# Four graph layers on one core: when the destination one-hots are written, and where the edge features are multiplied in

## The reference, cut

```
x = LN(x + gin(x))      # 3 x: agg = segment_sum(x[src], dst); two 64x64 linears
h = relu(concat(x[src], edge_attr) @ W1 + b1)          # 64+32 -> 128, per edge
h = h @ W2 + b2
agg = segment_sum(h, dst) / max(count(dst), 1)         # scatter_mean
x = LN(x + relu(concat(x, agg) @ W3 + b3) @ W4 + b4)   # the edge network
x = LN(x + attention(x, src, dst))                     # softmax over a node's edges
x = LN(x + relational(x, src, dst, type, weight))
```

## Time and profile before

| | |
|---|---|
| median of 3 runs | 1974.95 us (1972.48 to 1977.16) |
| profiled execution | 1974.92 us, of which the span is 1973.6 us |
| filing, POOL's last indirect DMA | ends at 609 us |
| preparation with layer one's first aggregation | 594 to 918 us |
| layers one to three, rest | to 1065 us |
| edge network | 1080 to 1370 us |
| attention | 1377 to 1690 us |
| relational layer | 1700 to 1973 us |
| busy over the span | PE 65%, DVE 50%, POOL 41%, ACT 31% |

### The profile page before, as it was taken

The page is one execution under the profiler, slowest core; times in us unless marked ns, Lnnn a source line. Parts: engine busy times, 40 slices in busy tenths (PEclk is TensorE's granted clock), DMA queues, the critical chain, the costliest instruction groups (busy, mean ns, idle before and its releaser), DMA issues.

```text
span 1973.6 us, 48209 instructions
## 1 busy us (share of the span) xinstructions
PE 1286.1 (65%) x20479; PEld 1175.4 (60%) x20480; DVE 979.0 (50%) x2196; ACT 618.1 (31%) x1433; POOL 806.2 (41%) x883
## 2 busy tenths in 40 slices
PE   6410000000002777778998999998799998989897
PEld 2300000000001666667897999998799998888896
DVE  7200020000001455554447555655788888888986
ACT  4000000000001777774213444343566666300000
POOL 1777777777772000000001444441010010388896
PEclk7555555555555999999997999998899999899999
DMA  7610000001102999997665788874666661344442
GB/s 230 241 35 15 15 15 14 13 14 48 34 14 75 349 357 359 352 346 272 239 253 198 279 302 310 312 293 176 255 242 238 224 244 52 141 165 158 170 177 89
DMA packets 89277, 360.69 MB, mean 183 GB/s; under 512 B 24940, under 2 KB 38431, under 8 KB 82079
## 3 DMA queue, kind: packets, MB, share of 16 engines
q1 hardware_dynamic: 75744, 349.84, 47.9%
q0 software_dynamic: 13312, 7.69, 1.7%
HBM read 250.77 MB, written 106.68 MB: 181 GB/s over the span
## 4 chain that ended last, share of the span: by engine, by line
PE 38%; another core or an unknown queue 22%; DVE 14%; issue 11%; ACT 7%; DMA 3%; POOL 2%; SPq 2%; ACTq 0%; DVEq 0%; POOLq 0%
PE ps L2923 8%; PE ps L2575 6%; PE ps L2911 6%; PE ps L3189 5%; PE ps L3542 4%; DMA arena<-recs 2%; DVE arena L2354 2%; PE ps L3556 2%; ACT arena L2479 2%; ACT arena L2531 2%; DVE arena L3607 2%; SPq L2264 2%; PE ps L2459 1%; POOL arena L3598 1%
## 5 line engine op out<-in xcount | busy, mean ns | idle before, releaser
L2174 POOL DMA_INDIRECT recs<-arena x416 | 425.6, 1023 | 173.2 <-issue 131.8
L2981 POOL CAST arena<-arena 128x512 f32<-128x512 bf16 (+1 forms) x175 | 119.2, 683 | 627.1 <-DMA arena<-hot_out 457.6
L2302 DVE TENSOR_TENSOR arena<-arena 128x25 f32<-128x25 int32 x25 | 4.9, 196 | 415.9 <-DMA arena<-recs 391.7
L3542 PE MATMUL ps<-arena 125*128 125x64 bf16 x5850 | 191.7, 194 | 8.8 <-issue 8.7
L2459 PE MATMUL ps<-wz,arena 32*128 32x128 f32 x1248 | 58.8, 319 | 208.9 <-ACT arena L2479 113.9
L3542 PEld LDWEIGHTS ps<-arena 125*128 125x128 bf16 x5850 | 186.5, 98 | 10.4 <-issue 9.9
L2923 PE MATMUL ps<-arena 128*128 128x125 f32 x1300 | 182.2, 282 | 0.0
L2459 PEld LDWEIGHTS ps<-wz,arena 32*128 32x128 f32 x1248 | 49.2, 215 | 221.1 <-ACT arena L2479 119.6
L3067 DVE TENSOR_TENSOR arena<-ps,arena 128x512 f32<-128x512 f32 (+1 forms) x175 | 114.3, 653 | 118.7 <-PE ps L2911 115.6
L3014 ACT ACTIVATE arena<-arena 128x512 f32<-128x512 f32 (+1 forms) x175 | 105.1, 601 | 171.8 <-DVE arena L3067 171.8
L2923 PEld LDWEIGHTS ps<-arena 128*128 128x128 f32 x1300 | 158.8, 192 | 0.0
(11 more groups left out here) (380 smaller groups left out, 2480.5 us busy)
## 6 DMA issues: line engine op xcount, KB each, us to landing
arena<-ids_out SPq DMA_DIRECT2D x100, 832.0 KB, 6.2
arena<-hot_out SPq DMA_DIRECT2D x75, 832.0 KB, 6.2
arena<-e_out SPq DMA_DIRECT2D x25, 1664.0 KB, 6.9
arena<-adj_out SPq DMA_DIRECT2D x41, 800.0 KB, 6.8
e_out<-arena SPq DMA_DIRECT2D x25, 1024.0 KB
hot_out<-arena SPq DMA_DIRECT2D x25, 832.0 KB, 7.6
adj_out<-arena SPq DMA_DIRECT2D x25, 800.0 KB, 5.8
e_out<-arena SPq DMA_DIRECT2D x25, 640.0 KB
```

Of the source, the lines that this page charges most:

```text
L2174: nc.gpsimd.indirect_dma_start(out=recs, out_offset=bass.IndirectOffsetOnAxis(ap=slot_row[:, t:t + 1], axis=0), in_=rec_in[:, t, :], in_of ...
L2981: nc.gpsimd.tensor_copy(hot_e[s % NH][:, 0:len(js), :], hot_in[d % 2][:, js[0]:js[0] + len(js), :])\
L3542: ins = M(bank(step % 4, C, k * C), hot_r[d % 2][r][0:NP_, j * SLOTS:(j + 1) * SLOTS], px3[:, block_of(d, j), piece, r * C:(r + 1) * C], s ...
```

## The change

1. *Destination one-hots early.* A new pair `sp_hot_ahead` and `dve_hot_ahead` goes over all 25 blocks while POOL still files: load the records once more, make the destination one-hots (26 tiles in one instruction), store them in `hot_out`. It stands in step 1 of SP's and DVE's streams, ahead of the load of block 2, and starts when half of the edges are filed, since its buffers lie over the first half of `rec_in`. The store of `hot_d` in the steps goes; DVE still makes `hot_d` there for the adjacency.
2. *Features stored instead of their product.* The halves L2459, their evictions, `e1_out` and the late product of block 24 go. The transposed features (448 KB a block) are stored in `attr_out`. ACT packs the next block's features after the fourth adjacency group instead of after all seven. The adjacencies rotate over four banks.
3. *Edge network.* PE adds the features' product into the same PSUM bank as the gather, in K=32 float32 matmuls of `attr_in` (`pe_sums`). Four steps are now issued together, in four rounds: up to four feature products on different rows, then the gathers of these tiles. ACT applies relu straight from PSUM, DVE splits the result into three parts (two subtractions a step), and PE sums by destination with the bf16 one-hot as weights and 3x128 columns moving. DVE reduces the three parts and scales, PE transposes, ACT copies into `agg`. POOL's casts go.

```diff
@@ sp_shadow
-                    while ahead < NA and ahead + 2 <= d and (ahead + 1) * NT * SLOTS // 2 <= filed:
+                    while ahead < NA and ahead + 2 <= d:
+                        if ahead == 0:
+                            for half in range(2):
+                                sp.wait_ge(sem(f"hot_stored{half}"), 16 * (NT // 2 + 1 - half))
...
+                if step == 1:
+                    sp_hot_ahead(sp)
...
-                    sp.wait_ge(sem("hot"), 3 * d + 3)
-                    sp.dma_start(hot_out[d], hot_d[d % 2].rearrange("p j n -> p (j n)"))\
-                        .then_inc(sem(f"hot_stored{d % 2}"), 16)
...
-                    if d < NT - 1:
-                        sp_e1(sp, d)
+                    sp.wait_ge(sem("attr_turned"), d + 1)
+                    sp.dma_start(attr_out[d], attT[d % 2]).then_inc(sem(f"attr_stored{d % 2}"), 16)
@@ new
+        def sp_hot_ahead(sp):
+            for c in range(2 * QUARTER // CHUNK - 2, 2 * QUARTER // CHUNK):
+                sp.wait_ge(sem(f"filed{c % 2}"), 16 * CHUNK * (c // 2 + 1))
+            for d in range(NT + 1):
+                if d < NT:
...
+                    if d >= 2:
+                        sp.wait_ge(sem("hot_ahead"), d - 1)
+                    sp.dma_start(dst_rec[d % 2], block_rows(d)).then_inc(sem(f"dst_in{d % 2}"), 16)
+                if d >= 1:
+                    sp.wait_ge(sem("hot_ahead"), d)
+                    sp.dma_start(hot_out[d - 1], hot_ahead[(d - 1) % 2].rearrange("p j n -> p (j n)"))\
+                        .then_inc(sem(f"hot_stored{(d - 1) % 2}"), 16)
@@ act_shadow
-                    if d < NT - 1:
-                        act_e1_half(act, d, 0)
-                        act_pack(act, d + 1)
-                        act_e1_half(act, d, 1)
+                        if g == 3 and d < NT - 1:
+                            act_pack(act, d + 1)
@@ pe_edge2
-                if step < G7:
...
-                    if step >= 4:
-                        pe.wait_ge(sem("e1_added"), step - 3)
...
+                if step < G7 and step % 4 == 0:
+                    pe_sums(pe, step)
...
-                    pe.wait_ge(sem("dst_hot"), s + 1)
-                    pe.wait_ge(sem("act_relued"), s + 1)
+                    pe.wait_ge(sem("act_low"), s + 1)
...
-                        ins = M(bank(4 + d % 2, NP_), act_out[s % 4][:, k * HID:(k + 1) * HID],
-                                hot_e[s % NH][:, k, 0:NP_], start=j == 0, stop=j == NT, skip_group_check=True)
+                        ins = M(bank(4 + d % 2, PIECES * HID)[0:NP_, :], hot_in[d % 2][:, j, 0:NP_],
+                                x[:, :, k * HID:(k + 1) * HID], start=j == 0, stop=j == NT, skip_group_check=True)
...
+                    if step == turn_step(d):
+                        pe.wait_ge(sem("agg_scaled"), d + 1)
...
+        def turn_step(d):
+            return 7 * (d + 1) + LAG + 2
@@ pe_sums: waits
+            pe.wait_ge(sem("src_hot"), d + 1)
+            pe.wait_ge(sem(f"attr_in{d % 2}"), 16 * (d // 2 + 1))
+            if first:
+                pe.wait_ge(sem("act_relued"), first)
@@ dve_edge2
-                    V.tensor_tensor(pre[step % 2][:, 0:m], bank(step % 4, m),
-                                    e1_in[d % 2][:, 4 * g * HID:4 * g * HID + m], ALU.add).then_inc(sem("e1_added"), 1)
+                    dve.wait_ge(sem("act_relued"), step + 1)
+                    V.tensor_tensor(x[:, 1, 0:m], x[:, 0, 0:m], hi(x[:, 0, :])[:, 0:m], ALU.subtract)\
+                        .then_inc(sem("act_left"), 1)
+                    dve.wait_ge(sem("act_left"), step + 1)
+                    V.tensor_tensor(x[:, 2, 0:m], x[:, 1, 0:m], hi(x[:, 1, :])[:, 0:m], ALU.subtract)\
+                        .then_inc(sem("act_low"), 1)
...
+                    V.tensor_reduce(agg_sum, bank(4 + d % 2, PIECES * HID)[0:NP_, :]
+                                    .rearrange("p (t f) -> p f t", t=PIECES), AX, ALU.add).then_inc(sem("agg_summed"), 1)
...
+                    V.tensor_scalar(agg_mean[d % 2], agg_sum, deg[:, 2, d:d + 1], None, ALU.mult)\
+                        .then_inc(sem("agg_scaled"), 1)
```

More of the change, by code:

```diff
@@ L283, in build @@
         e1_in0_at = e2_at.at
-        e1_in = [e2_at([128, SB * HID]) for _ in range(2)]
+        attr_in = [e2_at([128, 7 * SLOTS]) for _ in range(2)]
+        act_out += [e2_at([128, PIECES, 4 * HID])]
+        assert e2_at.at <= e1_in0_at + SB * HID
+        e2_at.at = e1_in0_at + 2 * SB * HID
         src_hot_at = e2_at.at
@@ L287, in build @@
         rcp_at = e2_at.at
-        rcp_row = [e2_at([128, CH * NP_]) for _ in range(2)]
+        agg_sum, agg_mean = e2_at([NP_, HID]), [e2_at([NP_, HID]) for _ in range(2)]
+        e2_at.at = rcp_at + 2 * CH * NP_
         p3_at = e2_at.at
@@ L291, in build @@
         assert e2_at.at >= sh.at
-        pre = [e2_at([128, 4 * HID]) for _ in range(2)]
+        e2_at.at += 2 * 4 * HID
         low_end, high_end = e1_at.at, e2_at.at
@@ L2325, in dve_shadow @@
                         .then_inc(sem("seg_made"), 1)
+                if step == 1:
+                    dve_hot_ahead(dve, chain)
                 if 2 <= step <= NT + 1:
@@ L2816, in hid_step, with px_sums @@
         def hid_step(c):
-            return 7 * (tiles(c)[-1] + 1) + LAG + 2
+            return 7 * (tiles(c)[-1] + 1) + LAG + 4
+        def turn_step(d):
+            return 7 * (d + 1) + LAG + 2
+        def px_sums(first):
+            cells = [(s, (s - first + i) % 4) for i in range(4) for s in range(first, min(first + 4, G7))]
+            cells = [(s, k) for s, k in cells if k < len(groups(s // 7)[s % 7])]
+            last = {s: at for at, (s, k) in enumerate(cells)}
+            done, at = [0] * len(cells), 0
+            for s in sorted(last):
+                at = max(at, last[s])
+                done[at] += 1
+            return cells, done
         OUT, EVICT, ROOT, SCALED, TURN, TURNED, HUP, HIGH, LEFT, MID, LOW = 3, 4, 9, 11, 13, 15, 17, 19, 21, 23, 25
@@ L3010, in act_edge2 @@
                     m = HID * len(groups(d)[g])
[L3011 to L3014 removed]
+                    act.wait_ge(sem("px_got"), step + 1)
+                    if step >= 5:
+                        act.wait_ge(sem("act_summed"), step - 4)
+                    A(act_out[step % 5][:, 0, 0:m], bank(step % 4, m), ACT.Relu)\
+                        .then_inc(sem("act_relued"), 1)
+                for d in range(NT):
+                    if step == turn_step(d):
+                        act.wait_ge(sem("agg_turned"), d + 1)
+                        A(agg[:, d * NP_:(d + 1) * NP_], bank(4 + d % 2, NP_, PIECES * HID), ACT.Copy)\
+                            .then_inc(sem("agg_read"), 1)
                 for c in range(NCH):
```

246 lines of the change are left out of this document (99 added, 147 removed).

## The result

The changed kernel takes **2062.2 us** (median, 2053.4 to 2069.2) against 1973.9 of the kernel before in the same call: ratio 1.044, interval 1.041 to 1.046, slower. The forecast was 2026 us with a range of 1958 to 2072. The profiled execution is 2053.4 us with a span of 2051.6.

What follows compares the result with a forecast made beforehand. It took filing as bound by POOL, the preparation by transfers and their loop, the edge network by PE. The sum 1974.9 - 32.8 - 6.1 + 88.5 + 2 = 2026.5 was said as 2026 us, range 1958 to 2072.

Steps and rivals of the forecast that it cites:

- Filing: While POOL files edges: making 25 destination tables on DVE costs POOL about 6 us, ends 0 and 12.
- The rival in which POOL waits for each whole table: Filing: POOL waits while DVE makes each table, +41 us, 2067 us; chance 0.03.
- Head start of block 2: Start of the preparation: block 2's adjacency is stored at 639.3 instead of 649.0, -10 us.
- Period: Preparation: 10.7 us a block instead of 11.92, ends 10.2 and 11.5; counted as 23.5 us saved.
- the loop named: Preparation: load landing, ACT's pack, last three evictions, adjacency store, then the next load; sum 10.4 us, taken as 10.7.
- The rival at 8.5 us a block: Preparation: landings are hidden from ACT, a loop of 17 us for two blocks decides; 1978 us; chance 0.10.
- Late product: Block 24's 14 float32 matmuls, which stood on the chain, go: -6.1 us.
- PE's own work in the edge network: Edge network: PE's work without waits is 12.33 us a block, 1.09 more than before.
- the lone round: Edge network: a round of feature products alone among full-height gathers costs 0.41 us, 7 rounds a block, 2.87 us.
- The sums: Edge network: PE's sums by destination, 384 columns a tile, take 0.164 us a tile, 4.26 a block.
- Waits: Edge network: new PE waits of 2.45 us a block (ends 0.4 and 3.5), transpose 1.55, source table 0.5, estimated rest 0.4.
- The clock: Edge network rival: granted clock falls to a mean of 0.90 as PE pauses, +34 us, 2060 us; chance 0.12.

Runs made afterwards that it cites:

- e4: The changed kernel with ACT packing the next block's features behind all seven adjacency evictions; 2033.7 us, ratio 1.030 to before.
- e7: The changed kernel with the transpose two steps later, the source table one step earlier and the pack behind all adjacency evictions; 1965.3 us on a chip of the second sort.
- e5: The kernel before with only the destination one-hots made and stored while edges are filed; 1949.2 us, ratio 1.166 to before on its chip.
- e6: The changed kernel with SP loading the records one block earlier, ahead of the adjacency store of the block before; 1979.4 us on a chip of the second sort.
- e1: The changed kernel with the transpose of the block's mean two steps later in the order; 2017.3 us, ratio 1.021 to before.
- e3: The changed kernel without feature products in the edge network and without the waits between their rounds; 1982.8 us, ratio 1.003 to before.
- e9: The kernel of e5 with SP loading the records one block earlier; 1950.5 us.
- e12: The kernel before, unchanged, run once more with a profile on another chip; 1669.5 us.

## Why the prediction was right

The direction, the place and the mechanism held: the gain in the preparation, the larger loss in the edge network, PE idle there behind DVE's scaling and source table. The size was low by 36 us (27 by the profiled execution).

- **Filing.** +6 forecast, +1.2 came (609.20 for 607.96), and that it came so near is luck. The price of 1 us of POOL for 8 of DVE, from one place, was too low: a table beside POOL's DMAs costs it more than half its own length. A table and the POOL issue beside it, after, and an issue of before:

```profile
353.71 1.89 DVE L2294 TENSOR_TENSOR arena<-iota,arena 128x3328 bf16<-128x3328 bf16 x1
```

```profile
353.78 2.67 POOL L2182 DMA_INDIRECT recs<-arena  x1 [0.30 <-issue]
```

```profile
477.33 1.09 POOL L2174 DMA_INDIRECT recs<-arena  x1 [0.31 <-issue]
```

After, 32 of the 416 issues take more than 1.00 us, together 28.5 us over the usual 0.97, each of them beside work of DVE. 25.5 of these stand beside the 24 tables made while POOL files (45.5 us). Before, 176 issues took more than 1.00 us, together 24.9, most of them 1.09 like the one shown and beside no DVE work at all, and nine longer pauses added 5.4. These are gone after, so the end moved little; why they are gone isn't shown. The rival in which POOL waits for each whole table didn't come in the time (+41), but more than half of what it says of a table did.
- **Head start of block 2.** -10 forecast, -3.6 came (645.44 for 649.03). "Block 1 is nearly through when the filing ends" was wrong: its adjacency is stored at 635.36. ACT's pack, which stands in front of block 1's last evictions, waits until 627.02 for the load that SP issues at 621.58, behind `sp_hot_ahead`, and the last evictions come only at 634.97. The load isn't all of it: e4, with the pack behind the evictions, stores block 1 at 635.21, where ACT's last evictions again come late, and e7, the same there on a chip of the second sort, at 619.12.
- **Period.** 10.7 forecast, (871.85 - 645.44) / 22 = 10.29 came, and the loop named was the right one: ACT waits for the load in front of the pack, and e4 and e6 take that wait away and gain. Altogether -39.4 against -32.8. With e5 it can be divided: of the 1.6 us of a block 0.3 go with the one-hots' transfers and the remaining 1.3, by difference, with the product, its loop and the other changes there. I had counted the bytes of both and seen the loop, but not which of the two the loop hung on. The rival at 8.5 us a block wasn't what the change does, but e6 shows 7.6 once the load is moved, so its loop of 17 us for two blocks was priced too high.
- **Late product.** -6.1 forecast, 48.2 - 39.4 = 8.8 came between the last adjacency and the edge network.
- **PE's own work in the edge network.** 12.33 forecast, 13.25 measured (e7). The mis-sized term is the lone round: 0.41 taken, 0.54 measured, 0.91 us a block. I had taken the 0.18 us for getting in and out of a long stretch for that of a lone round, which is 0.31 (0.54 - 0.23). Why it is more isn't shown. The sums were right: 0.164 us a tile forecast, 1.36 us for eight seen (0.17).
- **Waits.** 2.45 forecast, about 40.2 / 24 = 1.7 measured: transpose 1.2 for 1.55, table 0.36 for 0.5, relu 0.1.
- **The clock**, a rival of 0.12, came in part beside the forecast: 0.95 in the edge network. 13.25 / 0.95 is 0.7 us more. 13.25 + 1.7 + 0.7 = 15.65 of the 15.81. The rival's mechanism, PE pausing, agrees with e1 and e7, where fewer waits go with 0.98 and 1.00, and with e3, where more go with 0.94.
- **Start of the edge network**, not in the sum: from its first matmul to the end of block 0 it takes 32.7 us, before 17.9, so +15. Its first rounds run at 0.81 us instead of 0.50, PE waits 1.7 for the first subtractions, and all four steps of a burst are ready together.

Sum of what came: -48.2 + 14.8 + 24 x 4.57 + 1.1 = 77.3 us; the first matmul of attention stands 77.4 us later (1454.08 for 1376.66), and the span is 78.0 longer. The forecast missed 48.2 - 38.9 = 9 us of gain and 35 us of loss (90.5 for 125.5). So in part errors of both signs cancelled: too much loss was put down for waits and filing and too much gain for the head start, too little loss for PE's work, the clock and the start of the stage.

What the forecast didn't see at all is that the filing's idle time belongs to the chip: on the other two chips before had no idle time there to give away.

## What to carry to other kernels

Before filling an idle stretch, ask what keeps the engine idle there. If it is the supply of instructions and not the data, another chip may not have the idle time, and a queue that blocks for the whole stretch (SP in `sp_hot_ahead`) then costs the overlap: 278 us in e5. Look for the one load whose issue stands behind the stores of the block before; moving it gave 60 us in e6, where the transfers of a block had been halved before (353 GB/s at 11.92 us, 203 GB/s at 10.29) for 1.6 us; and it gave nothing while another loop (e9) held the period. Among others a small group of matmuls in another tile shape cost 0.54 us and not the 0.23 of a long run, so price it by itself. And a stage's end that hardly moves doesn't show that an addition was free: look at the single instructions beside it.

## What the runs showed of the hardware that I had not expected

- PE gets few instructions through while POOL issues indirect DMAs: 8 float32 matmuls in 22.4 us on one chip, while POOL issues one DMA in 1.26 us, and on another chip the same program runs 3542 matmuls in 552 us of that stage (e12). The kernel before is 1974 us on the one, 1670 us on that other and 1671 us on a third.
- A lone round of four 32-row float32 matmuls with 128 columns costs 0.54 us among full-height ones; four rounds in a row with a wait between them 0.58 each; without waits, in banks of their own, 0.23.
- The granted clock went down with PE's pauses: 1.00 with PE never idle and with 0.5 us of waits in a block of 13.7 (e7), 0.95 with 1.7 us in a block of 15.8.
- A one-hot table of 1.89 us on DVE costs POOL, while it issues indirect DMAs, about 1.1 us: 25.5 us for 24 tables.
